# Graph attention over 8192 nodes: the two rows of a pair go to one partition

## What is computed

```
h = input @ W
e = (h @ a1)[:, None] + (h @ a2)[None, :]
e = where(e > 0, e, 0.2 * e)
e = where(adj > 0, e, NEG)
attention = softmax(e, axis=1)
h_prime = attention @ h
out = layernorm(x + elu(h_prime), axis=-1)
```

## Time and profile before

| | |
|---|---|
| time, median of 3 runs | 746.89 us (745.5 to 748.28) |
| profiled execution | 748.48 us, span 746.6 us |
| busy share of the span | PE 78%, DVE 72%, ACT 69%, POOL 59% |
| DMA engines | busy in every slice but the last four |
| moved | 285.57 MB, 383 GB/s over the span |

### The profile page before, as it was taken

The page is one execution under the profiler, slowest core; times in us unless marked ns, Lnnn a source line. Parts: engine busy times, 40 slices in busy tenths (PEclk is TensorE's granted clock), DMA queues, the critical chain, the costliest instruction groups (busy, mean ns, idle before and its releaser), DMA issues.

```text
span 746.6 us, 11767 instructions
## 1 busy us (share of the span) xinstructions
PE 583.2 (78%) x3030; PEld 363.7 (49%) x3063; DVE 534.8 (72%) x2033; ACT 518.3 (69%) x418; POOL 437.2 (59%) x678
## 2 busy tenths in 40 slices
PE   3738898777886988787777788777789889887563
PEld 1214555554554555554444555554556556554452
DVE  3516778877788678777778877777777777787733
ACT  4356587866788677777788877777678887776111
POOL 2104566656667565666667666666666776665632
PEclk9977789988899889999999999998888888899755
DMA  8999999999999999999999999999999999995000
GB/s 346 324 429 422 429 425 422 427 424 421 400 411 411 416 414 429 427 427 427 427 426 427 428 425 426 428 429 426 428 398 410 401 428 428 429 424 223 18 22 15
DMA packets 34822, 285.57 MB, mean 383 GB/s; under 512 B 5880, under 2 KB 14224, under 8 KB 18416
## 3 DMA queue, kind: packets, MB, share of 16 engines
q1 hardware_dynamic: 20976, 272.70, 87.1%
q0 software_dynamic: 5120, 8.42, 3.2%
q10 hardware_dynamic: 8704, 4.20, 1.9%
HBM read 283.18 MB, written 4.19 MB: 385 GB/s over the span
## 4 chain that ended last, share of the span: by engine, by line
DMA 31%; PE 30%; DVE 15%; ACT 11%; SPq 5%; issue 4%; POOL 2%; ACTq 0%; DVEq 0%; POOLq 0%
DMA adj_sb<-in_adj 31%; PE fold L611 15%; ACT adj_squared L504 10%; PE x_att_ps L659 4%; SPq L372 4%; PE misc L636 3%; PE small L645 2%; DVE row_edge L858 2%; PE fold L609 1%; DVE dot L886 1%; PE x_att_ps L662 1%; DVE lead L821 1%; PE h_ps L671 1%; DVE below_end L854 1%; PE small L626 1%
## 5 line engine op out<-in xcount | busy, mean ns | idle before, releaser
L504 ACT ACTIVATE adj_squared<-adj_sb 128x4096 bf16<-128x4096 int32 x128 | 461.8, 3609 | 30.1 <-DMA adj_sb<-in_adj 30.1
L611 PE MATMUL fold<-adj_sb,bit_ident 128*128 128x512 bf16 x1024 | 304.9, 448 | 12.2 <-DMA adj_sb<-in_adj 8.7
L459 POOL DMA_INDIRECT nb<-in_x,index x160 | 165.2, 1032 | 111.0 <-issue 66.2
L611 PEld LDWEIGHTS fold<-adj_sb,bit_ident 128*128 128x128 bf16 x1024 | 110.3, 108 | 152.1 <-issue 62.9
L808 DVE MAX8 top_map<-fold 128x8 f32<-128x512 f32 x128 | 87.9, 697 | 48.4 <-PE fold L611 46.6
L348 POOL TENSOR_SCALAR edge_row<-row_iota,edge_in 128x128 f32<-128x128 int32 x186 | 112.9, 618 | 0.0
L609 PE MATMUL fold<-col_no,ident_bf 128*128 128x512 bf16 x96 | 38.6, 402 | 89.5 <-DMA adj_sb<-in_adj 89.3
L439 POOL TENSOR_SCALAR empty_diag<-ident,counts 128x128 f32<-128x128 f32 x64 | 49.0, 770 | 94.6 <-PE x_att_ps L662 68.0
L524 ACT ACTIVATE y_out<-y,shift,rstd 128x128 f32<-128x128 f32 x64 | 28.1, 486 | 82.6 <-POOL shift L430 82.6
L609 PEld LDWEIGHTS fold<-col_no,ident_bf 128*128 128x128 bf16 x128 | 15.9, 124 | 124.7 <-issue 87.3
L659 PE MATMUL x_att_ps<-spread,nb 128*128 128x128 f32 x384 | 64.2, 310 | 6.5 <-POOL spread L418 6.5
(11 more groups left out here) (107 smaller groups left out, 702.4 us busy)
## 6 DMA issues: line engine op xcount, KB each, us to landing
adj_sb<-in_adj SPq DMA_DIRECT2D x128, 2048.0 KB, 12.1
out<-y_out ACTq DMA_DIRECT2D x32, 128.0 KB, 13.7
nb<-in_x,index POOLq DMA_INDIRECT x160, 6.3
W_sb<-in_L_gnn_W SPq DMA_DIRECT2D x1, 64.0 KB, 1.9
x_sb<-in_x SPq DMA_DIRECT2D x4, 0.5 KB, 17.2
a_sb<-in_L_gnn_a SPq DMA_DIRECT2D x2, 0.5 KB, 2.1
```

What stands on the lines that cost most here:

```text
L459: nc.gpsimd.indirect_dma_start(out=nb_of(j, g)[:, c, :], out_offset=None, in_=x[:, :], in_offset=bass.IndirectOffsetOnAxis(ap=index[:, g, ...
L504: nc.scalar.activation(adj_squared[:, h % 2, :], adj_sb[:, h % LOAD_SLOTS, :], ACT.Square, accum_out=half_sum[:, h:h + 1]).then_inc(square ...
L611: last = nc.tensor.matmul(fold[:, h % LOAD_SLOTS, :], bit_ident[:, b, :], adj_low[:, h % LOAD_SLOTS, b * FOLD:(b + 1) * FOLD, 0], start=Fa ...
```

## The change

The rows of a step, 256 neighbouring ones, are dealt to the partitions in pairs: partition p holds rows 2p and 2p+1 of the step, the even one in the step's first tile, the odd one in its second. Row j\*256 + 2p + t now lies in partition p of tile 2j + t.

- The adjacency slices stay 128 runs of 16 KB. The rows of one slice now lie 64 KB apart in memory, not 32 KB, and a step's two tiles interleave.
- In the load of `x` a partition reads two neighbouring rows at a time: runs of 1 KB, not 512 bytes, half as many of them.
- A store writes two neighbouring rows from each partition: 128 runs of 1 KB, not 256 runs of 512 bytes.
- `row_id` is filled with the new numbers, and `row_place`, one more iota of 128 x 2, takes its part in `sent`.
- In the loop for rows that don't fit, the adjacency row is read straight into the new layout, which saves one transposition by PE and its copy.

```diff
-    adj_tiles = adj.rearrange("(t p) c -> t p c", p=P)
-    out_tiles = out.rearrange("(t p) c -> p t c", p=P)
-    x_tiles = x.rearrange("(t p) c -> p t c", p=P)
+    adj_tiles = adj.rearrange("(j p t) c -> j t p c", p=P, t=PAIR)
+    out_tiles = out.rearrange("(j p t) c -> j p t c", p=P, t=PAIR)
+    x_tiles = x.rearrange("(j p t) c -> p j t c", p=P, t=PAIR)
...
+        x_pairs = x_sb[:].rearrange("p (j t) c -> p j t c", t=PAIR)
...
-                Q = TILES // 4
+                Q = TILES // PAIR // 4
...
-                        tile = adj_tiles[bass.ds(i * BODY + h // 2, 1), :, (h % 2) * HALF:(h % 2 + 1) * HALF]
+                        tile = adj_tiles[bass.ds(i * GROUPS + g, 1), h // 2 % PAIR, :, (h % 2) * HALF:(h % 2 + 1) * HALF]
...
-                            nc.sync.dma_start(x_sb[:, q * Q:(q + 1) * Q, :],
-                                              x_tiles[:, q * Q:(q + 1) * Q, :]).then_inc(x_loaded[q], 16)
+                            nc.sync.dma_start(x_pairs[:, q * Q:(q + 1) * Q, :, :],
+                                              x_tiles[:, q * Q:(q + 1) * Q, :, :]).then_inc(x_loaded[q], 16)
...
-                nc.gpsimd.iota(row_id[:], pattern=[[P, TILES]], base=1, channel_multiplier=1).then_inc(iotas_ready, 1)
+                nc.gpsimd.iota(row_id[:].rearrange("p (j t) -> p j t", t=PAIR), pattern=[[P * PAIR, TILES // PAIR], [1, PAIR]],
+                               base=1, channel_multiplier=PAIR).then_inc(iotas_ready, 1)
+                nc.gpsimd.iota(row_place[:], pattern=[[P, PAIR]], base=1, channel_multiplier=1).then_inc(iotas_ready, 1)
...
-                    nc.scalar.dma_start(out_tiles[:, bass.ds(j * BODY + g * PAIR, PAIR), :],
+                    nc.scalar.dma_start(out_tiles[bass.ds(j * GROUPS + g, 1), :, :, :].rearrange("o p t c -> (o p) t c"),
                                         y_out[:, g, :, :]).then_inc(out_stored[g], 16)
...
-                dve.wait_ge(iotas_ready, 7)
+                dve.wait_ge(iotas_ready, 8)
...
-                nc.vector.tensor_copy(sent[:, :, ROW_COL], row_id[:, 0:PAIR])
+                nc.vector.tensor_copy(sent[:, :, ROW_COL], row_place[:])
```

More of the change, by code:

```diff
@@ L121, in graph_attention @@
         row_id = sb("row_id", [P, TILES], i32)
+        row_place = sb("row_place", [P, PAIR], i32)
         offset = sb("offset", [P, P], i32)
@@ L213, in graph_attention @@
         key_bc = sb("key_bc", [P, 1], fp32)
-        adj_row = sb("adj_row", [TILES, P], i32)
+        adj_row = sb("adj_row", [P, TILES], i32)
         x_row = sb("x_row", [1, D], fp32)
@@ L220, in graph_attention @@
         r_x = sb("r_x", [P, 1], fp32)
-        mask = sb("mask", [TILES, P], fp32)
-        maskT = sb("maskT", [P, TILES], fp32)
+        mask = sb("mask", [P, TILES], fp32)
         r_score = sb("r_score", [P, TILES], fp32)
@@ L385, in _ @@
                         row = sp.value_load(this_row[0:1, 0:1], min_val=0, max_val=N - 1)
-                        nc.sync.dma_start(adj_row[:], adj[bass.ds(row, 1), :].rearrange(
-                            "o (c q) -> (o c) q", q=P)).then_inc(row_loaded, 16)
+                        with nc.allow_non_contiguous_dma(reason="one row of the adjacency, in pairs"):
+                            nc.sync.dma_start(adj_row[:].rearrange("p (j t) -> p j t", t=PAIR),
+                                              adj[bass.ds(row, 1), :].rearrange("o (j p t) -> (o p) j t", p=P, t=PAIR)
+                                              ).then_inc(row_loaded, 16)
                         nc.sync.dma_start(x_row[:], x[bass.ds(row, 1), :]).then_inc(row_loaded, 16)
@@ L730, in _ @@
                     with pe.Fori(0, n) as r:
-                        hold(pe, row_to_pe, r * 6 + 1, pe_spare)
+                        hold(pe, row_to_pe, r * 5 + 1, pe_spare)
                         nc.tensor.transpose(misc[0:1, 0:P], key_max[:], ident[:]).then_inc(pe_to_row, 1)
@@ L735, in _ @@
                                          ).then_inc(pe_to_row, 1)
-                        hold(pe, row_to_pe, r * 6 + 2, pe_spare)
+                        hold(pe, row_to_pe, r * 5 + 2, pe_spare)
                         nc.tensor.matmul(misc[:, P + 1:P + 2], ones[0:1, :], r_s[:], start=True, stop=True
                                          ).then_inc(pe_to_row, 1)
[L739 to L742, removed]
+                        hold(pe, row_to_pe, r * 5 + 3, pe_spare)
                         nc.tensor.transpose(misc[0:1, 0:P], r_max[:], ident[:]).then_inc(pe_to_row, 1)
-                        hold(pe, row_to_pe, r * 6 + 5, pe_spare)
+                        hold(pe, row_to_pe, r * 5 + 4, pe_spare)
                         nc.tensor.matmul(misc[:, P:P + 1], ones[0:1, :], r_negmax[:], start=True, stop=True
@@ L752, in _ @@
                         last.then_inc(pe_to_row, 1)
-                        hold(pe, row_to_pe, r * 6 + 6, pe_spare)
+                        hold(pe, row_to_pe, r * 5 + 5, pe_spare)
                         nc.tensor.matmul(h_ps[0:1, 0, 0:D], r_x[:], W_sb[:], start=True, stop=True
@@ L1043, in _ @@
                         nc.vector.reduce_max(key_max[:], key[:], AX.X).then_inc(row_to_pe, 1)
-                        hold(dve, pe_to_row, r * 8 + 1, dve_spare)
+                        hold(dve, pe_to_row, r * 7 + 1, dve_spare)
                         v.after(nc.vector.reduce_max(this_key[:], misc[0:1, 0:P], AX.X))
                         nc.vector.tensor_scalar(this_row[:], this_key[:], -1.0, None, ALU.add).then_inc(row_picked, 1)
-                        hold(dve, pe_to_row, r * 8 + 2, dve_spare)
+                        hold(dve, pe_to_row, r * 7 + 2, dve_spare)
                         v.after(nc.vector.tensor_copy(key_bc[:], misc[:, P:P + 1]))
@@ L1053, in _ @@
                         nc.vector.reduce_sum(r_s[:], x_dot[:], AX.X).then_inc(row_to_pe, 1)
-                        hold(dve, pe_to_row, r * 8 + 3, dve_spare)
+                        hold(dve, pe_to_row, r * 7 + 3, dve_spare)
                         v.after(nc.vector.tensor_copy(s_bc[:], misc[:, P + 1:P + 2]))
-                        nc.vector.tensor_scalar(mask[:], adj_row[:], 0.0, None, ALU.is_gt).then_inc(row_to_pe, 1)
+                        v.after(nc.vector.tensor_scalar(mask[:], adj_row[:], 0.0, None, ALU.is_gt))
@@ L1057, in _ @@
                         v.after(nc.vector.tensor_scalar(r_score[:], t_all[:], s_bc[:, 0:1], None, ALU.add))
[L1058 to L1062, removed]
+                        v.after(nc.vector.scalar_tensor_tensor(r_lrelu[:], r_score[:], ALPHA, r_score[:],
+                                                               ALU.mult, ALU.max))
@@ L1063, in _ @@
+                        nc.vector.tensor_scalar(r_neg[:], mask[:], -NEG, NEG, ALU.mult, ALU.add)
+                        v.after(nc.vector.tensor_tensor(r_e[:], r_lrelu[:], mask[:], ALU.mult))
                         v.after(nc.vector.tensor_tensor(r_e[:], r_e[:], r_neg[:], ALU.add))
                         nc.vector.reduce_max(r_max[:], r_e[:], AX.X).then_inc(row_to_pe, 1)
-                        hold(dve, pe_to_row, r * 8 + 5, dve_spare)
+                        hold(dve, pe_to_row, r * 7 + 4, dve_spare)
@@ L1066, in _ @@
                         nc.vector.tensor_reduce(r_negmax[:], misc[0:1, 0:P], AX.X, ALU.max, negate=True
                                                 ).then_inc(row_to_pe, 1)
-                        hold(dve, pe_to_row, r * 8 + 6, dve_spare)
+                        hold(dve, pe_to_row, r * 7 + 5, dve_spare)
                         nc.vector.tensor_copy(r_negmax_bc[:], misc[:, P:P + 1]).then_inc(row_to_act, 1)
-                        hold(dve, pe_to_row, r * 8 + 7, dve_spare)
+                        hold(dve, pe_to_row, r * 7 + 6, dve_spare)
```

2 lines of the change are left out of this document (1 added, 1 removed).

## The result

Over ten runs each the changed kernel took 751.41 us and the kernel before 747.08 us; the ratio is 1.0055, 95% interval 1.0035 to 1.0075. Forecast were 742.9 us, with a range of 739.5 to 748.5. The profiled execution took 750.95 us with a span of 749.1 us. Every ratio in this text, with its 95% interval, is formed from all runs of both kernels in one set, so it can differ by some 0.2% from the quotient of the medians.

What follows compares the result with a forecast made beforehand. The stream of DMA packets was taken to set the pace. 2.35 us from x and 1.65 us from the stores, with adjacency and the rest at zero, made 4.0 us: median 742.9 us, range 739.5 to 748.5 us.

Steps and rivals of the forecast that it cites:

- What bounds the kernel: Whole stream: DMA packets set the pace, a step's transfers summing to 20.63 us against a period of 20.58 us.
- The load of x: Start of the kernel: half of the 8192 runs go, and with them half the excess, a gain of 2.35 us.
- The agreement of 9.2 and 9.0 ns: Excess per run in the load of x and in the stores, taken as showing a cost per run, not per packet.
- The stores: 27 stores beside the stream: half the runs go, 0.072 us a store, a gain of 1.65 us.
- the slow parts: 184.5 to 287 and 533 to 594.5 us, at 412 and 406 GB/s: put down to PE's clock at half.
- The adjacency: Slices of 16 KB runs, pitch from 32 to 64 KB: 614 ns a run as before, term zero.
- The rest: One more iota on POOL, 0.17 us, covered at the start: zero, or 0.2 us without that cover.
- The third: Rival, adjacency slices: the wider pitch slows reads; over 0.5% slower from about 1.25% on, 755.4 us at 2%; chance 0.13.
- The second rival: Load of x and stream: nothing comes of it, packet bytes set the rate or gains return as waiting; 746 to 747 us, chance 0.25.
- the even part: Stretch between the slow parts at 427 GB/s, read from 307 to 512 us; a step of 20.5 us forecast there.
- The tail: From the last slice's landing, taken as 679.3 us, to the end: 67 us of compute, forecast to stay.

Runs made afterwards that it cites:

- the best one: Changed kernel with row_place declared last and 128 unused bytes ahead of each of x_sb, nb and y_out: 739.35 us, ratio 0.9888.

## Why the prediction was wrong

**What bounds the kernel: right.** The step's time followed its packets. Of the 0.37 us by which a step got longer, the sorted packets account for 0.29 to 0.35, by how the unclear ones are laid: some 0.22 us behind gathers, 0.06 to 0.08 behind a gather's closing packet (625 to 630 ns for 612), 0.04 to 0.08 in the other runs and the gathers' own packets, less 0.03 in the store.

**The load of x: right in size, by luck, and wrong in its reason.** 2.35 us were forecast; 14.4 - 11.9 is 2.5 us. But the excess was mostly not a cost per run. Nor did the packets stay at 2 KB: 3.51 MB in 3479 packets is 1 KB each, so packets and runs changed together. `x_sb` lies 128 bytes past a multiple of 256; aligned, a packet of four 512 byte runs takes 89 ns and not 119, at 383 GB/s. The agreement of 9.2 and 9.0 ns, on which I built, was chance. Of the 9.2 some 7 belong to the address. Of the 9.0 only some 4.6 are there from start to start: 23.6 ns, less the 19.0 that 512 bytes take within a 16 KB run (607 ns from start to start).

**The stores: nearly twice too much.** 0.072 us a store were forecast and the shares give 4.51 - 3.69 us over ten, 0.08 us. But shares count the ends of packets that overlap the next one. From start to start a store shrinks by 38 ns only: 0.7 us over the 19 stores outside the slow parts, 1.0 over all 27, so 1.65 us should have been about 0.9. By themselves the paired stores gave a ratio of 0.9979 (0.9955 to 1.0003), which can't be told from no change.

**The adjacency: the pitch is free, as forecast, and the term was still wrong.** This is the step that failed: "The number and size of runs stay [...] I take the same", 614 ns. It became 625. The term had only the pitch as a reason to change; it left out what lies ahead of a run on its engine and where `nb` starts. With the buffers at their old place the kernel took 743.18 us, 3.6 us less than the kernel before in its set (its ratio leaves 1.5 to 6 us open), so the gains were there in sum, for the 4.0 forecast. The 32 bytes under `nb` cost 7.0 us in the kernel before (753.79 against its 746.82 in the same set), 8.2 us in the changed one (751.41 against 743.18, from two sets), and turned the gain into a loss.

**The rest: the missed line.** I priced the added iota at its 0.17 us on POOL and looked no further. The diff shows a new buffer declared in the middle of the list; the order of declarations sets all addresses behind it. The prediction asked whether the instructions depend on the new rows, and never where the buffers would lie.

**The rivals.** The third named the right side, with a chance of 0.13 and the pitch as its mechanism. Its sign came true, with 16 KB runs over 618 ns, and still its mechanism is refuted by two versions: 64 and 128 KB gave ratios of 1.000 and 0.999. (The Trainium skill, "DMA: Bandwidth & Descriptors", section "Latency and other measured facts", prices pitches from 512 KiB on, and none of these runs goes there.) The second rival, that 1 KB runs bring nothing over runs of 512 bytes, was dismissed with 291 against 431 GB/s; that difference was mostly not one of size, since 512 byte runs into an aligned buffer reach 383 GB/s and there the pairing brings `x` nothing.

The Trainium skill has a rule that could have warned: "DMA: Bandwidth & Descriptors", section "How a descriptor splits into AXI transactions", says that a descriptor, which moves one run, is cut into transactions of 256 bytes. A transaction can read less, but it must start at a multiple of 256, so a 512 byte row that starts elsewhere goes in three pieces and not in two. The page words this of reads, and doesn't say that it holds for the side in SBUF that is written, which is the one that moved here. The runs agree on the 256: 32, 64 and 128 off are alike, 256 is as good as 0. They don't show what the page lets expect of size: the gather's own packets grew by 4 ns only, and it is the run behind them that pays some 50 ns. For a 16 KB run one piece more of 65 would be 9 ns, an estimate from the page's rule and the 611 ns; the best runs take 611 ns either way. And the stores, which read `y_out`, take the same off a multiple of 256 and on one. Why the run behind a gather pays stays open.

**The slow parts.** I put them down to PE. That wasn't tested, but it isn't what the trace says either: the DMA view of the kernel before from 184 to 287 us has

```profile
DMA packets 4936, 42.44 MB, mean 412 GB/s; under 512 B 849, under 2 KB 2133, under 8 KB 2466
...
q1 hardware_dynamic: 2776, 40.47, 94.0%
```

and by the reckoning above the 16 KB runs themselves took 94.0% of 103 us x 16 / 2470 = 627 ns there, beside 614 in the even part. The packets say more: the median run takes 611 ns in both parts, but in the slow one 99 of 2470 runs take over 700 ns, the longest 2.3 us, where in the even part 1 of 5099 does. The engines didn't run out of slices; single packets were held up. Such parts come in nearly all kernels at other times, in the best one for one stretch only (412 GB/s at 164 to 205 us). What holds the packets up stays open.

**The tail.** 68.9 us from the last slice waited for (680.2 us) to the end, for 67.3: 1.5 us of the profiled execution's loss lie there, and I have no cause for them. The prediction took 679.3 us for the landing of the last slice, but it is that of the last but one; the last lands at 684.2 us, and at 684.9 after the change. From there to the end it is 62.4 and 64.2 us, and 60.5 to 66.8 over the traces of all versions, so the difference is within what this part varies by.

```profile
668.67 11.58 DMA adj_sb<-in_adj
```

## What to carry to other kernels

A new buffer is part of a change even where it is 8 bytes that take up 32: look at what its declaration moves, and above all at where the targets of small DMA writes start. Put buffers that DMAs write in small rows at multiples of 256 bytes, and declare small new ones last. Where a stream of packets sets the pace, sort them by what went before: a loss that shares and means spread over everything had one kind of neighbour here.

## What the runs showed of the hardware

- A gather that writes to a buffer that starts off a multiple of 256 bytes costs the packet behind it: with 512 byte rows 32, 64 or 128 bytes off, the next 16 KB run on that engine takes 659 to 670 ns instead of 620 to 624, with 160 gathers of 128 rows 0.7 to 1.1% of this kernel.
- Into `x_sb`, 128 bytes off, a packet of four 512 byte runs took 119 ns, aligned 89; a 1 KB packet 51, aligned 46.
- Rows of 16 KB that lie 32, 64 or 128 KB apart are read at the same 426 to 427 GB/s.
- A store of 1 KB runs takes 42.4 ns a packet from start to start, one of 512 byte runs 23.6, with the buffer in SBUF off a multiple of 256 bytes or on one.
- SP issued a DMA of 128 runs in 0.43 us (median of 64), one after another at about 141 GB/s with 65.5 KB each; 64 such requests in place of 4 cost 10.9 us (757.93 against 747.06).
